# One-hots four at a time, and the first linear layer of each graph layer moved into the neighbour product

## The reference, cut to what matters

```python
# network 2: sum of edge rows by source node
edge_aggr = zeros(n, HIDDEN).at[row].add(edge_features)
# network 4, five layers
for l in range(5):
    agg = jax.ops.segment_sum(h[src], dst, num_segments=N)
    rst = h + agg
    x = rst @ W1[l] + b1[l]
    x = jax.nn.relu(_bn(x, bn1_g[l], bn1_b[l]))
    x = x @ W2[l] + b2[l]
    x = jax.nn.relu(_bn(x, bn2_g[l], bn2_b[l]))
    h = jax.nn.relu(_bn(x, bn3_g[l], bn3_b[l]))
```

## Time and profile before

| | |
|---|---|
| time, median of 3 runs | 11594.17 us (11581.43 to 11606.92) |
| the profiled execution's own time | 11670.47 us |
| its span | 11667.7 us |
| mean granted TensorE clock | 0.771 |
| PE / DVE / ACT / POOL busy | 57% / 38% / 28% / 39% |
| one of the five layers, start to start | 515 us |

### The profile page before, as it was taken

The page is one execution under the profiler, slowest core; times in us unless marked ns, Lnnn a source line. Parts: engine busy times, 40 slices in busy tenths (PEclk is TensorE's granted clock), DMA queues, the critical chain, the costliest instruction groups (busy, mean ns, idle before and its releaser), DMA issues. The chain is left out here.

```text
span 11667.7 us, 155049 instructions
## 1 busy us (share of the span) xinstructions
PE 6702.1 (57%) x38276; PEld 4877.6 (42%) x38277; DVE 4387.9 (38%) x13627; ACT 3232.3 (28%) x5782; POOL 4494.5 (39%) x4476
## 2 busy tenths in 40 slices
PE   1610002731276886466664666546665989898896
PEld 1610001720022785355563555545554444443443
DVE  3860001641298777444443444434445020202103
ACT  0000000001298675334343433434334010101001
POOL 1877776057600000466654666456664000000000
PEclk8555555755588998677786878878787989898998
DMA  5333333433333442233322333233331646464453
GB/s 91 105 92 101 94 99 107 125 95 110 112 119 114 141 127 63 54 67 69 68 64 64 69 69 69 57 69 69 68 68 41 194 133 202 127 193 137 146 179 115
DMA packets 1223091, 1192.27 MB, mean 102 GB/s; under 512 B 234919, under 2 KB 1108022, under 8 KB 1222440
## 3 DMA queue, kind: packets, MB, share of 16 engines
q1 hardware_dynamic: 826660, 630.69, 19.4%
q0 software_dynamic: 150784, 336.22, 11.7%
q10 hardware_dynamic: 245444, 222.71, 6.9%
HBM read 974.35 MB, written 217.29 MB: 102 GB/s over the span
## 5 line engine op out<-in xcount | busy, mean ns | idle before, releaser
L1194 POOL DMA_INDIRECT ring<-gat_rows,idx x2496 | 2416.5, 968 | 1775.6 <-issue 1491.1
L1319 PE MATMUL ps<-ring,xT_b 128*128 x8192 | 1387.9, 322 | 1339.2 <-ACT xT_b L1405 1017.0
L1319 PEld LDWEIGHTS ps<-ring,xT_b 128*128 128x128 f32 x8192 | 1225.1, 229 | 1459.3 <-issue 1457.3
L1367 DVE CUSTOM_DVE_ANT_0 xT_a<-ps,mask,xT_a 128x512 f32<-128x512 f32 x1024 | 769.1, 751 | 2511.7 <-remote 1707.1
L1309 PE MATMUL ps<-ident,s_col 128*128 128x128 f32 x8192 | 1306.6, 308 | 439.7 <-issue 392.5
L1397 ACT ACTIVATE xT_a<-xT_a,state 128x514 f32<-128x514 f32 x1024 | 742.4, 725 | 2644.7 <-DVE xT_a L1367 2083.6
L1309 PEld LDWEIGHTS ps<-ident,s_col 128*128 128x128 f32 x8192 | 1201.7, 222 | 471.7 <-issue 422.8
L1607 PE MATMUL ps<-xT_b,features 128*128 128x504 f16 (+1 forms) x5655 | 1195.1, 367 | 2.3 <-DVE xT_a L1627 2.3
L1469 PE MATMUL ps<-ring,xT_b 128*128 x2048 | 337.7, 344 | 1286.3 <-issue 1112.6
L1791 POOL TENSOR_TENSOR features<-xT_b,features 128x640 bf16<-128x640 f32 x50 | 82.5, 1654 | 2490.5 <-ACT features L1788 2490.1
L687 POOL DMA_INDIRECT by_src<-ring,state x832 | 880.0, 1058 | 286.5 <-issue 286.5
(11 more groups left out here) (376 smaller groups left out, 9046.7 us busy)
## 6 DMA issues: line engine op xcount, KB each, us to landing
dl_all<-dloc_rows ACTq DMA_DIRECT2D x1052, 128.0 KB
xT_b<-adjacency SPq DMA_DIRECT2D x145, 882.0 KB, 4.9
xT_b<-adjacency SPq DMA_DIRECT2D x145, 756.0 KB, 4.5
adj_tile<-adjacency SPq DMA_DIRECT2D x100, 882.0 KB
adjacency<-xT_b ACTq DMA_DIRECT2D x319, 252.0 KB
adj_tile<-adjacency SPq DMA_DIRECT2D x100, 756.0 KB
ring<-by_src SPq DMA_DIRECT2D x52, 1040.0 KB
ring<-gathered SPq DMA_DIRECT2D x208, 260.0 KB
```

The lines of the kernel that those rows point to most:

```text
L1194: pool.indirect_dma_start(ring[:, o:o + RC], None, table[:, :], bass.IndirectOffsetOnAxis(idx[g][:, u:u + 1], 0)).then_inc(q[f"rows{g}"], 16)
L1319: m = pe.matmul(bank(BO + v % 2, R), pw[v % 4][:, w * P:(w + 1) * P], ring[:, w * RC:][:, bass.ds(look(SLOT, u - 7), R)], start=w == 0, st ...
L1367: dve.tensor_tensor_reduce(out=m[:, 0:TE], in0=bank(BS + u % 4, TE), in1=mask[u % 4][:, :], scale=1.0, scalar=m[:, TE + 1:TE + 2], op0=ALU ...
```

## The change

1. In `source_sums` the four `tensor_scalar` of a step become one `tensor_tensor` over 128x512, with the node numbers repeated four times and four source columns spread over 128 each.
2. In `adjacency` the source one-hots are made by one `tensor_tensor` for four steps (AT1 = 4) into the same 16 buffers. It waits until four of them are free. The destination one-hots stay one `tensor_scalar` a step.
3. In `neighbours` the last small product goes window by window, with a semaphore count for each window, so that copies can start one by one. The first linear layer is computed from the copied window, 504 nodes at a time, by `first_weights`: for windows 0 to 6 inside the second part of the product, after every fifth block from block 14 on, and for windows 7 to 12 behind it. It uses banks 5 and 6, which part two leaves free. ACT adds the bias and writes the result over the window in `xT_a`, DVE takes the statistics, and `norm_affine` closes the phase. The separate `linear` phase goes.
4. The second linear layer now writes `xT_b`, and `split_features` works in `xT_a`. It also loads the first two tiles of the next product (KEPT = 2, the two `adj_tile` buffers), and SP waits for them before the barrier.

```diff
@@ -85,6 +85,7 @@
 AU = 16
 SU = 8
 AB = 16
+AT1 = 4
 AK = -(-(AT + NKEY - 1) // AU) * AU
 AJ = -(-AK // P)
 AKP = AJ * P
@@ -92,6 +93,7 @@
 assert NV * RUN == ET and NV % 2 == 0
 PAIRS = (NKEY + 1) // 2
 DW = 7
+KEPT = 2
 PAD_DST = NBP * P
 L2VECS = ("b", "g", "be")
 GVECS = ("b1", "b2", "bn1_g", "bn1_b", "bn2_g", "bn2_b", "bn3_g", "bn3_b")
@@ -1475,11 +1477,11 @@
                     dve.wait_ge(q["stage"], look(NEED, u))
                     if have(4):
                         dve.wait_ge(q["product"], n - 3)
-                    for w in range(W):
-                        m = dve.tensor_scalar(eqs[u % 4][:, w * P:(w + 1) * P],
-                                              node_ids[:, bass.ds(look(NODE, u), P)],
-                                              src_cols[:, w:][:, bass.ds(look(COL, u), 1)], None, ALU.is_equal)
-                    m.then_inc(q["eq"], 1)
+                    dve.tensor_tensor(
+                        eqs[u % 4].rearrange("p (w n) -> p w n", n=P),
+                        node_ids[:, bass.ds(look(NODE, u), P)].rearrange("p (a n) -> p a n", a=1).to_broadcast([P, W, P]),
+                        src_cols[:, bass.ds(look(COL, u), W)].rearrange("p (w a) -> p w a", a=1).to_broadcast([P, W, P]),
+                        ALU.is_equal).then_inc(q["eq"], 1)
                 if have(2):
                     v = (u - 2) % SU
                     st = S[:, bass.ds(look(BLOCK, u), D)]
@@ -1501,6 +1503,9 @@
             at0 = 3 * AKP + KEYJ * P
             wide = WD // 2
             node1 = [XTa[:, i * 64:i * 64 + 64].bitcast(BF16) for i in range(AB)]
+            node4 = [XTa[:, i * 64 * AT1:(i + 1) * 64 * AT1].bitcast(BF16).rearrange("p (t n) -> p t n", n=P)
+                     for i in range(AB // AT1)]
+            node_row = node_ids[:, 0:P].rearrange("p (a n) -> p a n", a=1).to_broadcast([P, AT1, P])
             node2 = [(ring[:, at0 + i * wide:at0 + (i + 1) * wide] if i < 12 else
                       XTa[:, AB * 64 + (i - 12) * wide:AB * 64 + (i - 11) * wide]).bitcast(BF16) for i in range(AB)]
             pair = lambda t, c: t.rearrange("p (k c) -> p k c", c=c)[:, :, 0:WD]
@@ -1518,9 +1523,11 @@
 
             def dve_body(n, u, have, look):
                 if have(AB):
-                    dve.wait_ge(q["product"], n - AB + 1)
-                dve.tensor_scalar(node1[u % AB], node_ids[:, 0:P], src_of[:, u:][:, bass.ds(n - u, 1)],
-                                  None, ALU.is_equal)
+                    dve.wait_ge(q["product"], n - AB + 1 + (AT1 - 1 if u % AT1 == 0 else 0))
+                if u % AT1 == 0:
+                    dve.tensor_tensor(node4[u // AT1], node_row,
+                                      src_of[:, u:][:, bass.ds(n - u, AT1)].rearrange("p (t a) -> p t a", a=1)
+                                      .to_broadcast([P, AT1, P]), ALU.is_equal)
                 dve.tensor_scalar(node2[u % AB], node_ids[:, 0:WD], dst_of[:, u:][:, bass.ds(n - u, 1)],
                                   None, ALU.is_equal).then_inc(q["eq"], 1)
 
@@ -1567,6 +1574,20 @@
             act.wait_ge(q["load"], 32)
             dve.tensor_copy(gcur[:, :], vec[:, bass.ds(l * len(GVECS) + VB["Gb10"], len(GVECS))])
             parts = [range(0, DW), range(DW, NWIN)]
+            width_of = lambda w: min(WD, NB * P - w * WD)
+            window = lambda w: XTa[:, w * WD:w * WD + width_of(w)]
+
+            def first_weights(w):
+
+                if w == 0:
+                    pe.wait_ge(q["load"], 32)
+                pe.wait_ge(q["evac"], max(w, 6) // 2 + 1)
+                pe.wait_ge(q["out"], (max(w, 6) + 1) // 2)
+                if w >= 2:
+                    pe.wait_ge(q["stage"], w - 1)
+                pe.matmul(bank(5 + w % 2, width_of(w)), wst(6), window(w), start=True, stop=True
+                          ).then_inc(q["mm"], 1)
+
             by_block = extra[:, :].rearrange("p (c b) -> p b c", b=NBP)
             for i in range(NB):
                 m = pe.matmul(PS[0:NV, 7 * 512:7 * 512 + 3 * D], by_block[:, i, :], H3[:, i * 3 * D:(i + 1) * 3 * D],
@@ -1593,10 +1614,9 @@
                     b = n % NT
                     if n >= NT:
                         sp.wait_ge(q["product"], n - NT + 1)
-                    sp.dma_start(tiles[b][:, 0:len(ws) * WD].rearrange("p (w c) -> p w c", c=WD),
-                                 adj[i * NWIN + ws[0]:i * NWIN + ws[-1] + 1, :, :].rearrange("w p c -> p w c")
-                                 ).then_inc(q[f"ld{b}"], 16)
-                    pe.wait_ge(q[f"ld{b}"], 16 * (n // NT + 1))
+                    if n >= KEPT:
+                        load_tile(i, ws, b)
+                        pe.wait_ge(q[f"ld{b}"], 16 * (n // NT + (b >= KEPT)))
                     for x in range(3):
                         h = H3[:, (i * 3 + x) * D:(i * 3 + x + 1) * D]
                         for j, w in enumerate(ws):
@@ -1611,23 +1631,32 @@
                                           start=False, stop=False)
                     m.then_inc(q["product"], 1)
                     n += 1
+                    if k and i % 5 == 4 and i // 5 - 2 in parts[0]:
+                        first_weights(i // 5 - 2)
                 if k == 0:
                     s.wait(pe)
-                for x in range(3):
-                    for w in ws:
-                        width = min(WD, NB * P - w * WD)
+                for w in ws:
+                    width = width_of(w)
+                    for x in range(3):
                         m = pe.matmul(bank(w % 8, width), part(V3, x), run_hit[0:NV, w * WD:w * WD + width],
                                       start=False, stop=x == 2)
-                m.then_inc(q["summed"], 1)
-            for w in range(NWIN):
-                width = min(WD, NB * P - w * WD)
-                to = XTa[:, w * WD:w * WD + width]
-                if w % 2 == 0:
-                    dve.wait_ge(q["summed"], 1 if w < DW else 2)
-                    dve.tensor_copy(to, bank(w % 8, width)).then_inc(q["evac"], 1)
-                else:
-                    act.wait_ge(q["summed"], 1 if w < DW else 2)
-                    act.activation(to, bank(w % 8, width), ACT.Copy).then_inc(q["out"], 1)
+                    m.then_inc(q["summed"], 1)
+            for w in parts[1]:
+                first_weights(w)
+            for ws in parts:
+                for w in ws:
+                    if w % 2 == 0:
+                        dve.wait_ge(q["summed"], w + 1)
+                        dve.tensor_copy(window(w), bank(w % 8, width_of(w))).then_inc(q["evac"], 1)
+                    else:
+                        act.wait_ge(q["summed"], w + 1)
+                        act.activation(window(w), bank(w % 8, width_of(w)), ACT.Copy).then_inc(q["out"], 1)
+                for w in ws:
+                    act.wait_ge(q["mm"], w + 1)
+                    act.activation(window(w), bank(5 + w % 2, width_of(w)), ACT.Identity, bias=gv["b1"]
+                                   ).then_inc(q["stage"], 1)
+                    stats_of(XTa, w, WD, min(WD, N - w * WD), "stage", w + 1)
+            norm_affine(gv["bn1_g"], gv["bn1_b"], NWIN, s)
             end_phase()
 
 
@@ -1750,12 +1779,22 @@
         s(dve, lambda: dve.memset(XTa[:, NB * P:], 0.0))
         end_phase()
 
+        def load_tile(i, ws, b):
+
+            sp.dma_start(tiles[b][:, 0:len(ws) * WD].rearrange("p (w c) -> p w c", c=WD),
+                         adj[i * NWIN + ws[0]:i * NWIN + ws[-1] + 1, :, :].rearrange("w p c -> p w c")
+                         ).then_inc(q[f"ld{b}"], 16)
+
         def split_features(first):
 
             groups = 2 * HALF
             of = lambda t, c, g, o=0: t[:, g * GB * c:(g + 1) * GB * c].rearrange("p (b c) -> p b c", c=c)[:, :, o:o + D]
             rest = [rows5[h][:, :].rearrange("p (b c) -> p b c", c=D) for h in range(2)] if first else \
-                [XTb[:, h * GB * D:(h + 1) * GB * D].rearrange("p (b c) -> p b c", c=D) for h in range(2)]
+                [XTa[:, h * GB * D:(h + 1) * GB * D].rearrange("p (b c) -> p b c", c=D) for h in range(2)]
+            for b in range(KEPT):
+                load_tile(b, range(0, DW), b)
+            for b in range(KEPT):
+                sp.wait_ge(q[f"ld{b}"], 16)
             if not first:
                 pe.sem_inc(q["mm"], 2 * GB)
                 dve.sem_inc(q["evac"], 2)
@@ -1778,7 +1817,7 @@
             for g in range(groups + 2):
                 if g < groups and not first:
                     act.wait_ge(q["mm"], (g + 1) * GB)
-                    act.activation(rows5[g % 2][:, :], XTa[:, g * GB * P:(g + 1) * GB * P], ACT.Relu, bias=aff[:, 1:2],
+                    act.activation(rows5[g % 2][:, :], XTb[:, g * GB * P:(g + 1) * GB * P], ACT.Relu, bias=aff[:, 1:2],
                                    scale=aff[:, 0:1]).then_inc(q["stage"], 1)
                 if 1 <= g <= groups:
                     act.wait_ge(q["evac"], g + ahead)
@@ -1797,9 +1836,8 @@
```

(5 more changed lines are left out.)

## The result

The changed kernel takes 11435.61 us (median of 3 runs, 11432.65 to 11465.88) against 11594.17: the ratio is 0.9871, with a 95% interval of 0.984 to 0.9902. The profiled execution took 11465.88 us with a span of 11464.6.

A forecast was written before the change was run, and what follows sets the result against it. DVE and PE bound the sums by turns, DVE and ACT the matrix, PE the layers' product, and gathers the first stretches. Layers 52, sums 15 and matrix 5 make 72 us: 11522 from 11594, range 11500 to 11545, eight in ten 11470 to 11570.

The forecast's parts named there:

- Layers: Five layers: 16.2 saved in the tail plus 0.9 less 6.6, 10.5 us each, 52 in all; bounds 32 to 59.
- Tail, window and period: In a layer: tail of 8.2 us in place of 24.4, 0.94 us a first_weights window, period of 504 to 505.
- the ledger: Layer sum: seven first_weights inside part two cost PE 7 x 0.94 = 6.6 us, against 16.2 and 0.9 gained.
- Sums: Sums without gathers: a turn gains about 0.5 us, 30 turns 15 us; bounds 6 to 45.
- PE with 10.29 us a turn caps it: Sums without gathers: DVE's step falls from 0.99 to 0.80 us, but PE's unbroken work limits the gain a turn.
- the slow rival: Large compare at two cycles an element, 1.14 us of DVE, in both one-hots; up to +190 us, 11785; chance 0.05.
- Matrix, without gathers: Count matrix's second stretch, DVE and ACT both near full: 0 us, between +10 and -15.
- Matrix, beside gathers: Count matrix's first stretch: 10 steps more, 5 us; bounds none to 40 steps, 20 us.
- so the pace is held by PE: Matrix beside gathers: DVE's instructions fall from five to about four a step, PE still issues five.
- PE's five at 0.7 are already 3.5 us: Matrix beside gathers: PE's five instructions fill the 3.5 us step, so the lower bound of the gain is none.
- My last sign of being wrong: Prediction wrong if the first stretches, which gathers fill, change pace for a reason the rows don't show.
- My 0.13 rival: All edits give more: sums in full, more steps beside gathers; 59 + 45 + 20 = 124 us, about 11470; chance 0.13.

The follow-up runs named there:

- late_first: Changed kernel with all 13 first_weights of a layer behind the product, none inside it: 9893.68 us, 0.9848 of the kernel before.
- the fillers: Ten unused float32 matmuls in PE's idle gap behind every eighth step of the sums, added to the kernel before: 9976.23 against 10049.69 us, ratio 0.9929.
- before_again: The kernel before, unchanged, run again for its trace: 10044.72 us.
- pad_dve: Changed kernel plus two DVE counts in each matrix step on a semaphore nobody waits for: 9899.3 us.
- fours: Changed kernel with the matrix's waits of PE and DVE and SyncE's rooms once for four steps: 9894.73 us, 0.9849 of the kernel before.
- sums_alone: Kernel before with only the one 128x512 compare in source_sums: 11640.74 against 11687.08 us, ratio 0.9959.
- before_again_2: The kernel before, unchanged, run once more for its trace on another chip: 11599.16 us.
- matrix_alone_2: Kernel before with only the adjacency edit (one compare for four steps), second run: 11570.23 against 11599.16 us, ratio 0.9975.
- matrix_pad_sp: Kernel before with only the adjacency edit, plus two SyncE counts a step on a semaphore nobody waits for: 11615.72 us, one execution.

## Why the prediction was wrong

**Layers: right.** 52 us forecast; 59 at the first level, 63 by differences at the second, and in the profile 10.5 to 12.5 a layer (periods of 504.9, 503.3, 504.0 and 502.9 us against 515.4, 515.2, 515.6 and 515.4). Tail, window and period came within 0.3, 0.08 and 1 us. (The tail's 8.2 counts 0.2 for each of the two hand-overs; with 0.2 once the terms give 8.0. The 0.2 was an estimate, and no row shows it.) `late_first` supports the ledger: the windows inside cost nearly what they would cost behind.

**Sums: the term was mis-sized at the step "PE with 10.29 us a turn caps it".** 15 us forecast, at most 45; 46 measured at the first level, with 17 us lost in unchanged layers, and 65 by differences at the second. DVE's compare and its first steps were right to 0.01 us; the two cycles an element of the slow rival, 1.14 us a compare, no run shows (0.69 in the profile after). But I took PE's 10.29 us for work of a fixed length, though the earlier trace rows showed a clock of 0.76, and asked neither when in a turn the clock was low nor whether the edit would change it. It takes 8.75 on average after the edit. Over some 29 turns the clock is 1.51 x 29 = 44 us, and the shorter gap 0.40 x 29 = 12, which is what I had forecast as 0.5 a turn. The rest is steps beside the gathers, where I had nothing: 24 in place of 18 in the profile after. The kernel before spends 6 us of a turn at a granted clock of 0.50 behind its idle gap, the changed one 2.8, 3.4 or none. That a gap of that kind costs the clock is shown by the fillers (0.76 to 0.97 over the stretch beside the gathers); why turns behind gaps of 2.9 to 3.1 us lose half as much as those behind 3.3, or nothing, is not.

**Matrix, without gathers: right.** 0 forecast; the pace is 0.47 us on either side, once both stretches are cut where the gathers end.

**Matrix, beside gathers: wrong for the level of the result, at "so the pace is held by PE".** 5 us forecast with 20 as the upper bound. It holds at the first level, near which the profile before was taken: 0 us. At the second, where the times of the result belong, PE's 0.70 us was no constant, and the edit gives 29 by itself (16 to 42 by its interval) and 40 by differences. I made a bound from "PE's five at 0.7 are already 3.5 us", a duration that was not fixed (a median of 701 ns in the earlier trace rows, 37 in the profile after), and from a median of two kinds of durations, which the least and the most in the earlier trace rows (5 and 1423 ns) could have told me. My last sign of being wrong, first stretches that change their pace for a reason that the rows don't show, is what came. At the third it gives some 50 us of phase because POOL's gathers go faster (590 of them and their stores 612.25 us in `before_again`, 552.77 in `pad_dve`), which no step of mine held. My 0.13 rival named the direction (fewer DVE instructions, more steps) but stopped at 20.

**The sum.** 63 + 65 + 40 = 168 at the second level against 72: of the 96 us missing, 50 are in the sums, most of them the clock, 35 the matrix beside the gathers, 11 the layers. The differences of medians that this rests on are good to some 20 us each. The assumption that the 76 us between the profiled execution and the median would stay fell too: the execution after lies 30 above its median.

**Still open:** why the share of 0.7-us instructions differs by level, and why it falls for PE at the second level, and not at the first, when DVE issues fewer; whether fewer waits on PE (`fours`) would help at the first two levels, since the runs landed at the third; and why unchanged layers take 17 us more in `sums_alone`.

## What to carry to other kernels

Before a stretch in which one engine works "without a break" is taken as its bound, read the granted clock inside one turn of the loop. Here it started at 0.50 behind an idle gap of 3.33 us; of the 1.91 us that a turn gained the clock was 1.51 and the shorter gap 0.40, and idle matmuls that fill the gap gave the kernel before 73 us. A duration beside the gathers is no price: the same address instruction of PE has a median of 699 ns in `before_again_2` and 37 in `matrix_alone_2` and in `before_again`; bound a change in such a stretch from "no long ones left", not from its median. And where phases differ between two profiles in code that did not change, ask first at which level each of them was taken (the kernel before takes 11687, 11595 or 10050 us), and read the unchanged phases of a single edit too before its time is taken as its worth: of `sums_alone`, 17 of 65 us were lost there.

## What the runs showed of the hardware that I had not expected

- Beside indirect gathers the register and semaphore instructions of PE, DVE and SyncE that the traces hold take about 0.70 us, twice that, or nearly nothing (PE's addresses in `before_again_2`: least 3, median 699, most 1410 ns; DVE's in the profile before: 4, 689, 1397; SyncE's counts in `matrix_pad_sp`: 3, 696, 1405). At the third level, with the same gathers, PE's all took 37 ns and the kernel was 13% faster (10050 against 11595 us).
- Ten unused float32 matmuls a turn, in PE's idle gap, made the kernel before 73 us faster (10049.69 to 9976.23).
- At the third level gathers took longer beside small 16-bit compares with one input than with one large compare of two inputs for four of them (1157 against 1031 ns a gather); in float32 it was the reverse (961 against 1036). At the second level the matrix's edit made POOL's time for the same 590 longer instead, 520.53 to 529.98 us.
